# Graph attention over three groups of edges instead of two: weighting half a group later, maxima chained on all 128 partitions, exponentials in a table of their own

## The chip, the cores and the metric

The kernel runs on one core of one Trainium2 chip, as one program. The metric is the device time of one execution in microseconds (us); what is compared is the median of several executions.

## The reference

Four graph layers over 3125 nodes with 256 features and 53125 edges sorted by their destination node. Layers 0 and 1 are normalized sums over edges (GCN). Layer 2 is a graph transformer of three sub-layers, layer 3 a graph attention. The change touches the attention that layer 2 (three times) and layer 3 (once) share, cut here to what matters (8 heads of 32 features):

```python
for l in range(L):                                   # L = 3
    ...
    scores = jnp.sum(q_dst * kt, axis=-1) / scale    # (edges, 8)
    scores = scores * mu[l].T[edge_type]
    m = jax.ops.segment_max(scores, dst, num_segments=N)
    e = jnp.exp(scores - m[dst])
    s = jax.ops.segment_sum(e, dst, num_segments=N)
    w = e / (s[dst] + 1e-10)
    agg = jax.ops.segment_sum(V[src] * w[..., None], dst, num_segments=N)
    attn = agg.reshape(N, D) @ Wo[l] + bo[l]
    x = _layer_norm(x + attn, ...)
    ...                                              # gelu MLP, layer norm
```

Layer 3 computes its scores from other terms, with a leaky relu, and then does the same maximum, exponential and sums.

## The kernel before, in words

**Tiles.** The edges are padded to 464 tiles of 128 edges (NT). Two tiles are a pair that belongs to one block of 128 destination nodes; four tiles are a quad, sixteen tiles (four quads, eight pairs) a group. There are 29 groups (WG). `attend` (L1396) handles all groups in order. It is called four times: `L2a0`, `L2a1`, `L2a2` (together L2a in the profile) and `L3a`.

**What one group needs.** GpSimd (POOL) gathers 16 times 128 rows of the table of keys and values by an indirect DMA (L1460), into a ring of 10 quads (11 in L3a). A slot of the ring is free once its quad has been weighted (`weighted_ready`). SyncE loads the one-hot matrices as bytes; ScalarE (ACT) widens them (`turn` L1709, `widen` L1717). TensorE (PE) multiplies the turned one-hots with the node features (`ask`, L1754, 4 matmuls a quad), which puts each edge's query into PSUM. VectorE (DVE) multiplies by the gathered key (`product`, L1513), reduces over the head (`reduce`, L1519; in L3a `join` adds a gathered term, L1533), and so has 16 x 8 scores.

**The maxima.** PE transposes the scores (`flatten`, L1774). DVE scans them up and down with penalties between segments (`scan_up` L1550, `scan_down` L1555), and spreads the two ends of each tile over a 128 x 32 table (`spread_ends` L1560). PE multiplies this table by `c.head` (128 x 8), so that the ends of all tiles stand in order on 8 partitions (`sequence`, L1779). DVE chains them up and down (`chain_up` L1566, `chain_down` L1572), starting from the group before. PE multiplies by `c.heads` (8 x 128) to spread the result over 128 partitions again (`expand`, L1784). DVE picks each partition's own tile (`pick_own` L1584, `join_own` L1589), raises the scans by it (L1593, L1598) and subtracts (`lower`, L1604). PE transposes back, and computes a factor for sums that started in an earlier group (`unflatten`, L1790 and L1792). ACT takes the exponentials (`soften`, L1729), which it writes straight into the 33rd column of each head of `weighted`, and DVE multiplies the gathered values by them (`weigh`, L1615, once a quad). PE sums each pair with the widened one-hots (`total`, L1765), DVE adds the sums to the accumulator in SBUF (`add`, L1544), and rescales one block (`rescale`, L1625).

**The order.** All is written out by hand: Python loops that are unrolled, one instruction stream for each engine, semaphores between them. In iteration n DVE interleaves the scores of group n with the maxima, the weighting and adds 0 to 2 of group n-1, and adds 3 to 7 of group n-2. After `spread_ends` DVE has one add and one product before `chain_up` waits for `sequence`; after `chain_down` it has a reduction and an add before `pick_own` waits for `expand`; after `lower` it has a product and an add before `weigh` waits for the exponentials. On PE, `total` of pairs 6 and 7 of group n-2 and `ask` of quads 2 and 3 of group n stand between these steps.

## Time and profile before

| | |
|---|---|
| median of 3 runs | 5554.59 us (5538.73 to 5557.21) |
| profiled execution, first to last instruction | 6456.7 us |
| TensorE busy, mean granted clock | 4457.4 us (69%), 0.831 |
| VectorE busy | 3832.0 us (59%) |
| GpSimd busy | 3364.1 us (52%) |
| ScalarE busy | 1605.5 us (25%) |

The profiled execution gives no time of its own beside its span, and the span is 902 us over the median of the runs: this execution was slower than those that are timed. Rows of the profile name an instruction by its source line, its engine, the tensors that it writes and reads, and their shapes; "idle before" is the time in which the engine had nothing to run just before the instruction. The granted clock is TensorE's, as a share of 2.4 GHz. The name of a releaser is inferred; "remote", or a DMA of another stage, stands where it was not found.

### The profile page before, as it was taken

How to read it: one execution, taken by the hardware profiler on the slowest of the kernel's cores; microseconds unless marked ns; L12 is line 12 of the kernel's file. 1: busy time of each engine (PE TensorE's matmuls, PEld its weight loads, DVE VectorE, ACT ScalarE, POOL GpSimd, SP SyncE). 2: the span in 40 equal slices, each digit the busy share in tenths (PEclk: the TensorE clock that was granted, in tenths of full speed). 3: DMA queues.
4: the chain of work that ended last, by engine and by line, in shares of the span. 5: the costliest groups of instructions: out<-in, count | busy, mean ns of one | idle time of the engine just before them, and what ended most of it. 6: DMA issues, size and time to landing. Idle time of an engine off the chain costs nothing. (4 is left out here: it accounts for less than half of the span.)

```text
span 6456.7 us, 68859 instructions
## 1 busy us (share of the span) xinstructions
PE 4457.4 (69%) x19341; PEld 3493.0 (54%) x19341; DVE 3832.0 (59%) x8692; ACT 1605.5 (25%) x3882; POOL 3364.1 (52%) x3108
## 2 busy tenths in 40 slices
PE   5666664577766666778857767796766679766776
PEld 4455453444436455557845555685555558545554
DVE  7544443544455666675347766643766776567777
ACT  3433332200004111113421211243211214312221
POOL 2588886366644555541356555134555530256663
PEclk9888887788888778779977777898778779878887
DMA  3688887255556555542266556315556541256664
GB/s 139 121 124 125 121 125 150 81 184 184 182 165 208 168 173 181 181 144 58 81 189 182 174 175 181 89 56 165 169 175 182 176 147 39 80 168 183 195 192 134
DMA packets 508435, 959.75 MB, mean 149 GB/s; under 512 B 85846, under 2 KB 298020, under 8 KB 507251
## 3 DMA queue, kind: packets, MB, share of 16 engines
q0 software_dynamic: 224512, 549.90, 34.1%
q1 hardware_dynamic: 283426, 404.92, 19.6%
q8 instruction: 170, 2.79, 0.2%
q14 instruction: 199, 1.62, 0.1%
q10 hardware_dynamic: 128, 0.52, 0.0%
HBM read 718.56 MB, written 236.50 MB: 148 GB/s over the span
## 5 line engine op out<-in xcount | busy, mean ns | idle before, releaser
L1460 POOL DMA_INDIRECT L2a_rows<-kv_rows,typed_index x960 | 966.3, 1007 | 627.8 <-DVE L2a_weighted L1615 349.9
L1765 PE MATMUL L2a_sums<-L2a_weighted,L2a_hot 128*128 128x264 f32 x2784 | 830.5, 450 | 166.8 <-DVE L2a_weighted L1615 159.4
L1754 PE MATMUL L2a_query<-x,L2a_turned 128*128 x2784 | 819.8, 447 | 55.8 <-ACT L2a_turned L1709 33.0
L867 POOL DMA_INDIRECT sum_rows<-L0s_rows,L0s_row_of x464 | 724.6, 1562 | 152.9 <-issue 119.4
L1765 PEld LDWEIGHTS L2a_sums<-L2a_weighted,L2a_hot 128*128 128x128 f32 x2784 | 591.2, 221 | 314.5 <-DVE L2a_weighted L1615 186.2
L1754 PEld LDWEIGHTS L2a_query<-x,L2a_turned 128*128 128x128 f32 x2784 | 627.2, 229 | 181.4 <-issue 62.5
L1460 POOL DMA_INDIRECT hold<-kv_rows,typed_index x432 | 445.4, 1031 | 449.8 <-DVE L2a_weighted L1615 279.5
L1460 POOL DMA_INDIRECT L3a_rows<-feature_rows,index x464 | 489.1, 1054 | 301.7 <-DVE L3a_weighted L1615 155.1
L1285 POOL DMA_INDIRECT L1s_rows<-rows,index x464 | 451.0, 972 | 351.2 <-issue 133.8
L1717 ACT ACTIVATE L2a_hot<-L2a_hot 128x512 f32<-128x512 uint8 x348 | 218.7, 629 | 1470.8 <-PE L2a_sums L1765 726.6
L1002 PE MATMUL L0s_message<-features,L0s_share 128*128 x928 | 312.8, 496 | 285.9 <-ACT L0s_share L967 285.9
L2296 POOL TENSOR_SCALAR L2d_here<-hold,mask 128x256 f32<-128x256 f32 x200 | 183.1, 933 | 552.6 <-DVE hold L2372 404.5
L1342 PE MATMUL L1s_code_ps<-L1s_wide,L1s_fields 128*128 128x512 f32 x464 | 285.8, 702 | 219.3 <-DVE L1s_code L1311 138.4
L1519 DVE TENSOR_REDUCE L2a_score<-L2a_prods 128x32 f32<-128x1024 f32 x348 | 417.8, 1201 | 0.4
L1002 PEld LDWEIGHTS L0s_message<-features,L0s_share 128*128 128x128 f32 x928 | 215.3, 242 | 364.9 <-issue 329.1
L1765 PE MATMUL L3a_sums<-L3a_weighted,L3a_hot 128*128 128x264 f32 x928 | 282.7, 457 | 92.6 <-DVE L3a_weighted L1615 89.3
L1709 ACT ACTIVATE L2a_turned<-L2a_turn 128x512 f32<-128x512 uint8 x348 | 216.9, 624 | 507.7 <-PE L2a_query L1754 191.8
L1513 DVE TENSOR_TENSOR L2a_prods<-L2a_query,L2a_rows 128x1024 f32<-128x1024 f32 x240 | 291.9, 1216 | 76.5 <-remote 47.3
L901 DVE TENSOR_TENSOR L0s_hot<-count,early 128x512 f32<-128x512 f32 x116 | 80.5, 694 | 419.0 <-ACT L0s_hot L980 412.7
L1305 DVE TENSOR_TENSOR acc<-acc,L1s_sums 128x256 f32 x232 | 97.4, 420 | 378.4 <-remote 176.5
L1544 DVE TENSOR_TENSOR acc<-acc,L2a_sums 128x264 f32 x696 | 290.4, 417 | 10.8 <-PE L2a_sums L1765 9.1
L1615 DVE TENSOR_TENSOR L2a_weighted<-L2a_rows,L2a_weighted 128x1024 f32<-128x1024 f32 x240 | 292.4, 1218 | 3.4 <-ACT L2a_weighted L1729 1.3
(428 smaller groups left out, 8550.9 us busy)
## 6 DMA issues: line engine op xcount, KB each, us to landing
code_rows<-L1s_code SPq DMA_DIRECT2D x116, 512.0 KB
L3a_code<-code_rows SPq DMA_DIRECT2D x116, 512.0 KB
L0s_wide<-source_rows SPq DMA_DIRECT2D x116, 256.0 KB
L2a_turn<-turned_rows SPq DMA_DIRECT2D x87, 256.0 KB
L2a_pens<-mask_rows SPq DMA_DIRECT2D x87, 256.0 KB
L2a_hot<-hot_rows SPq DMA_DIRECT2D x87, 256.0 KB
kv_rows<-L2d_key_rows SPq DMA_DIRECT2D x50, 384.0 KB, 2.6
kv_rows<-L2d_value_rows SPq DMA_DIRECT2D x150, 128.0 KB, 2.4
```

The lines of the kernel that those rows point to most:

```text
L867: pool.indirect_dma_start(c.sum_rows[u], bass.IndirectOffsetOnAxis(ap=row_of[:, 4 * n + u:4 * n + u + 1], axis=0), rows[n % ring][:, u, :] ...
L1002: last = pe.matmul(message[n % 2][:, u, :], share[n % 2][:, u, :], at(c.q, b[i])[:, 0:D], start=True, stop=True)
L1285: pool.indirect_dma_start(rows[n % ring][:, u, :], None, table, bass.IndirectOffsetOnAxis(ap=c.index[:, t:t + 1], axis=0)).then_inc(landed ...
L1342: pe.matmul(code_ps[j % 2][:, :, :].rearrange("p k d -> p (k d)"), fields[g % 2][:, :], wide[:, 2 * j % FT:2 * j % FT + 2, :].rearrange("p ...
L1460: pool.indirect_dma_start(rows[n % ring][:, u, :], None, table, bass.IndirectOffsetOnAxis(ap=index_of[:, t:t + 1], axis=0)).then_inc(lande ...
L1513: dve.tensor_tensor(prods[q % 2][:, :, :], query[q % 2][:, :, :], other, ALU.mult).then_inc(multiplied, 1)
L1519: last = dve.tensor_reduce(own.rearrange("p k h -> p (k h)"), prods[q % 2][:, :, :].rearrange("p k (h d) -> p (k h) d", h=H), AX.X, ALU.add)
L1544: dve.tensor_tensor(at(c.acc, b), at(c.acc, b), sums[(m * WP + j) % held][:, :], ALU.add).then_inc(added, 1)
L1615: dve.tensor_tensor(weighted[:, 4 * q:4 * q + 4, :].rearrange("p k (h d) -> p k h d", h=H)[:, :, :, 0:HD], rows[quad % ring][:, :, values: ...
L1717: act.activation(hot[quad % 2][:, :, :].rearrange("p u e -> p (u e)"), hot8[m % 2][:, q * 4 * P:(q + 1) * 4 * P], ACT.Copy).then_inc(hot_r ...
L1754: last = pe.matmul(query[q % 2][:, u, :], turned[quad % 2][:, u, :], at(c.q, b[2 * q + u // 2]), start=True, stop=True)
L1765: last = pe.matmul(sums[(m * WP + j) % held][:, :], hot[quad % 2][:, j % 2 * 2 + k, :], weighted[:, 2 * j + k, :], start=k == 0, stop=k == 1)
```

## The change

- `attend` is laid out over three groups. In iteration n (now 31 of them, before 30) DVE makes the scores of group n, the maxima of group n-1 and weights its quads 0 and 1, and weights quads 2 and 3 of group n-2, with all eight adds of that group. The three waits for PE and ACT get more work of DVE in front of them.
- `c.heads` becomes one 128 x 128 matrix (1 where two partitions have the same head), and `sequence` puts the ends on all 128 partitions. The chains run there on 128 x 32 instead of 8 x 32, `pick_own` reads them in SBUF, and `expand` with its two matmul passes is gone. The tables that it needs (`links`, `tail`, `apart`, `ends`) grow from 8 to 128 partitions.
- ACT writes the exponentials into one of two tables `prob`; `pour` (new, one a quad) copies them into `weighted`, which is now one tensor for each quad. `keep` (new) copies the rescaling factor from PSUM to SBUF.
- DVE loads 9 block numbers into registers at the start of an iteration instead of 16.

```diff
-        seq_ps = small[0:H, 2 * P:2 * P + 2 * WT]
-        tops_ps = small[:, 2 * P + 32:2 * P + 32 + 2 * WT]
+        seq_ps = small[:, 2 * P:2 * P + 2 * WT]
...
             def pick_own(m):
-                wait(dve, tops_ready, m + 1)
-                dve.tensor_tensor(pick[:, :, :], tops_ps.rearrange("p (u s) -> p s u", s=2), spread(c.each[:, :], 1, 2),
+                wait(dve, chained, 2 * m + 2)
+                dve.tensor_tensor(pick[:, :, :], tops[:, :].rearrange("p (u s) -> p s u", s=2), spread(c.each[:, :], 1, 2),
                                   ALU.mult).then_inc(picked, 1)
...
             def weigh(m, q):
                 quad = m * WQ + q
                 wait(dve, prob_ready, m + 1)
+                wait(dve, sums_ready, 2 * (quad - WQ + 1))
                 dve.tensor_tensor(
-                    weighted[:, 4 * q:4 * q + 4, :].rearrange("p k (h d) -> p k h d", h=H)[:, :, :, 0:HD],
+                    weighted[q][:, :, :].rearrange("p k (h d) -> p k h d", h=H)[:, :, :, 0:HD],
                     rows[quad % ring][:, :, values:values + D].rearrange("p k (h d) -> p k h d", h=H),
-                    weighted[:, 4 * q:4 * q + 4, HD::HC].unsqueeze(3).broadcast_to([P, 4, H, HD]), ALU.mult
-                ).then_inc(weighted_ready, 1)
+                    spread(prob[m % 2][:, 4 * q:4 * q + 4, :], 3, HD), ALU.mult).then_inc(weighted_ready, 1)
...
             dve.memset(c.acc[:, :, :], 0.0)
-            for n in range(WG + 1):
-                m = n - 1
+            for n in range(WG + 2):
+                m, k = n - 1, n - 2
+                more, chain, tail = n < WG, 0 <= m < WG, k >= 0
...
```

The order of DVE's steps in one iteration after the change, where all three groups are there: product(n,0), add(k,0), scan_up(m), add(k,1), scan_down(m), add(k,2), spread_ends(m), weigh(k,2), reduce(n,0), join(n,0), add(k,3), product(n,1), reduce(n,1), join(n,1), add(k,4), chain_up(m), add(k,5), chain_down(m), grow(m), pick_own(m), join_own(m), reach_first(m), reach_last(m), spread_fall(m), lower(m), weigh(k,3), product(n,2), reduce(n,2), join(n,2), product(n,3), reduce(n,3), join(n,3), add(k,6), add(k,7), weigh(m,0), rescale(m), weigh(m,1). ACT and PE:

```diff
             def soften(m):
-                if m >= 0:
-                    wait(act, below_ready, m + 1)
-                    wait(act, sums_ready, m * WP)
-                    act.activation(weighted[:, :, HD::HC], below_ps.rearrange("p (u h) -> p u h", h=H), ACT.Exp
-                                   ).then_inc(prob_ready, 1)
+                wait(act, below_ready, m + 1)
+                act.activation(prob[m % 2][:, :, :], below_ps.rearrange("p (u h) -> p u h", h=H), ACT.Exp
+                               ).then_inc(prob_ready, 1)
+
+            def pour(m, q):
+                quad = m * WQ + q
+                wait(act, prob_ready, m + 1)
+                wait(act, sums_ready, 2 * (quad - WQ + 1))
+                act.activation(weighted[q][:, :, HD::HC], prob[m % 2][:, 4 * q:4 * q + 4, :], ACT.Copy
+                               ).then_inc(poured, 1)
...
-                pe.matmul(seq_ps, c.head[:, :], ends[:, :, :].rearrange("p u s -> p (u s)"), start=True, stop=True
+                pe.matmul(seq_ps, c.heads[:, :], ends[:, :, :].rearrange("p u s -> p (u s)"), start=True, stop=True
                           ).then_inc(seq_ready, 1)
-
-            def expand(m):
-                wait(pe, chained, 2 * m + 2)
-                pe.matmul(tops_ps, c.heads[:, :], tops[:, :], start=True, stop=True).then_inc(tops_ready, 1)
...
+                    ask(n, 2, now)
+                if tail:
+                    total(k, 3)
                 if chain:
                     sequence(m)
-                total(m - 1, 7)
-                if more:
-                    ask(n, 2, now)
-                if chain:
-                    expand(m)
+                if tail:
+                    total(k, 4)
+                    total(k, 5)
                 if more:
                     ask(n, 3, now)
                 if chain:
                     unflatten(m)
-                total(m, 0)
-                total(m, 1)
+                if tail:
+                    total(k, 6)
+                    total(k, 7)
                 if ahead:
                     ask(n + 1, 0, near)
-                total(m, 2)
-                total(m, 3)
-                if ahead:
                     ask(n + 1, 1, near)
                 if more:
                     flatten(n)
-                total(m, 4)
-                total(m, 5)
-            for j in range(6, WP):
-                total(WG - 1, j)
+                if chain:
+                    total(m, 0)
+                    total(m, 1)
+                    total(m, 2)
```

## Rows read from the trace of the kernel before

**Rows 1.** The page: span, and busy time of each engine.

```profile
span 6456.7 us, 68859 instructions
PE 4457.4 (69%) x19341; PEld 3493.0 (54%) x19341; DVE 3832.0 (59%) x8692; ACT 1605.5 (25%) x3882; POOL 3364.1 (52%) x3108
```

**Rows 2.** Busy time by stretch: first and last call of `attend`, sum of all four.

```profile
core 0: us, PE busy (x) PEld busy (x) DVE busy (x) ACT busy (x) POOL busy (x), PEclk, DMA share, GB/s
2064.00:2911.00 847.00, 573.48 (x2086) 442.55 (x2086) 571.73 (x955) 159.99 (x290) 470.64 (x464) 0.79 0.57 171
...
5611.00:6433.00 822.00, 549.94 (x2086) 427.58 (x2086) 588.52 (x1100) 161.79 (x290) 489.13 (x464) 0.80 0.60 179
sum 3367.00, PE 2269.95 PEld 1754.89 DVE 2303.99 ACT 641.46 POOL 1900.79; mean PE 567.49 PEld 438.72 DVE 576.00 ACT 160.36 POOL 475.20
```

**Rows 3.** Groups of instructions, first L2a, middle (2172 to 2868 us): busy, mean ns, idle before.

```profile
L1460 POOL DMA_INDIRECT L2a_rows<-kv_rows,typed_index x275 | 278.2, 1012 | 188.1 <-DVE L2a_weighted L1615 108.8 <-issue 79.2
L1460 POOL DMA_INDIRECT hold<-kv_rows,typed_index x120 | 124.8, 1040 | 107.0 <-DVE L2a_weighted L1615 73.5 <-issue 33.5
L1566 DVE TENSOR_TENSOR_SCAN L2a_up<-links,L2a_up,L2a_small 8x32 f32<-8x32 f32 x25 | 6.7, 267 | 105.5 <-remote 91.7 <-issue 13.8
L1584 DVE TENSOR_TENSOR L2a_pick<-L2a_small,each 128x32 f32<-128x32 f32 x25 | 4.8, 192 | 98.1 <-DMA raw<-edge_rows 98.1
L1729 ACT ACTIVATE L2a_weighted<-L2a_small 128x128 f32<-128x128 f32 x25 | 10.0, 398 | 22.4 <-PE L2a_small L1792 22.2
L1723 ACT ACTIVATE L2a_fall<-L2a_gap,linked 8x1 f32<-8x1 f32 x25 | 6.9, 278 | 0.0
```

**Rows 4.** The same for L3a, middle (5700 to 6396 us).

```profile
L1460 POOL DMA_INDIRECT L3a_rows<-feature_rows,index x413 | 439.4, 1064 | 251.0 <-DVE L3a_weighted L1615 133.1 <-issue 117.9
L1615 DVE TENSOR_TENSOR L3a_weighted<-L3a_rows,L3a_weighted 128x1024 f32<-128x1024 f32 x104 | 126.9, 1220 | 36.4 <-ACT L3a_weighted L1729 35.9
L1584 DVE TENSOR_TENSOR L3a_pick<-L3a_small,each 128x32 f32<-128x32 f32 x26 | 5.0, 192 | 128.2 <-DMA L2a_rows<-kv_rows,typed_index 107.0 <-issue 21.3
```

**Rows 5.** Timeline, a group early in L2a: start, length, engine, line, [idle before].

```profile
2144.34 0.18 DVE L1560 TENSOR_TENSOR L2a_ends<-each,L2a_most 128x32 f32<-128x32 f32 x1
2144.44 0.42 DVE L1544 TENSOR_TENSOR acc<-acc,L2a_sums 128x264 f32 x1
2144.75 0.22 PE L1779 MATMUL L2a_small<-L2a_ends,head 128*8 128x32 f32 x2
2145.97 1.89 PE L1754 MATMUL L2a_query<-x,L2a_turned 128*128 x8
2153.60 0.27 DVE L1566 TENSOR_TENSOR_SCAN L2a_up<-links,L2a_up,L2a_small 8x32 f32<-8x32 f32 x1 [7.61 <-remote]
2156.59 0.19 DVE L1584 TENSOR_TENSOR L2a_pick<-L2a_small,each 128x32 f32<-128x32 f32 x1 [0.67 <-DMA raw<-edge_rows]
2156.81 0.19 DVE L1589 TENSOR_REDUCE L2a_other<-L2a_pick 128x2 f32<-128x32 f32 x1
2160.13 1.23 DVE L1615 TENSOR_TENSOR L2a_weighted<-L2a_rows,L2a_weighted 128x1024 f32<-128x1024 f32 x1 [0.37 <-ACT L2a_weighted L1729]
```

**Rows 6.** Timeline, the very first group of L2a: the two waits.

```profile
2127.43 0.19 DVE L1584 TENSOR_TENSOR L2a_pick<-L2a_small,each 128x32 f32<-128x32 f32 x1 [1.59 <-PE L2a_small L1784]
2131.79 1.22 DVE L1615 TENSOR_TENSOR L2a_weighted<-hold,L2a_weighted 128x1024 f32<-128x1024 f32 x1 [1.71 <-ACT L2a_weighted L1729]
```

**Rows 7.** Timeline, POOL and DVE a little later: gathers beside a weighting.

```profile
2162.74 1.22 DVE L1615 TENSOR_TENSOR L2a_weighted<-L2a_rows,L2a_weighted 128x1024 f32<-128x1024 f32 x1
2162.87 1.90 POOL L1460 DMA_INDIRECT L2a_rows<-kv_rows,typed_index  x1 [0.30 <-issue]
2165.08 0.95 POOL L1460 DMA_INDIRECT L2a_rows<-kv_rows,typed_index  x1 [0.31 <-issue]
```

**Rows 8.** The page's groups: gathers and scatters of layers 0 and 1.

```profile
L867 POOL DMA_INDIRECT sum_rows<-L0s_rows,L0s_row_of x464 | 724.6, 1562 | 152.9 <-issue 119.4 <-ACT L0s_rows L961 21.9 <-DMA sum_rows<-L0s_rows,L0s_row_of 11.6
L1285 POOL DMA_INDIRECT L1s_rows<-rows,index x464 | 451.0, 972 | 351.2 <-issue 133.8 <-ACTq L87 127.7 <-remote 62.1
```

183 lines of the change are left out of this document (93 added, 90 removed).

## The prediction

> **What bounds the kernel now.** I read the page first: VectorE and GpSimd are busy 59% and 52% of 6456.7 us, TensorE 69% [rows 1], so no engine is the bound by its share. By stretch, the four calls of the attention hold 3367 us of the span, and DVE works 2304 us of them [rows 2]. The groups of one call say where the other 1063 us are. In the middle of L2a, 25 groups of edges take 696 us, 27.8 each. DVE stands idle 105.5 us before the upward chain (L1566) and 98.1 before `pick_own` (L1584), 8.1 us a group, and next to nothing before anything else [rows 3]. In L3a it is 128.2 before `pick_own` and 36.4 before the weighting, 6.3 us a group of 26.4 [rows 4]. Both places wait for a small matmul of TensorE. The timeline shows how such a wait looks: the matmul of `sequence` is recorded at 2144.75 and 0.22 us long, the chain that waits for nothing else starts at 2153.60 [rows 5]. So PE signals far later than its record ends. POOL is no bound in this execution: of 696 us it waits 182 for a weighting to free its ring [rows 3].
>
> The Trainium skill (Perfetto Trace Analysis, Tensor Engine Instruction) says that a matmul's end in a profile is computed from its size, and that its signal comes after PSUM has acknowledged. The 8.6 us between those rows agree that the record does not tell the signal.
>
> **How this execution stands to the timed ones.** Its span is 902 us over the median of 5554.6, and no time of its own stands beside it. I must not book waits that the timed runs don't have. Taking all the waits named out of the attention gives back 84 x 8.14 + 28 x 6.3 = 861 us (28 full groups a call): 3367 - 861 = 2506, and with the 3090 us of everything else 5596. That is 41 us over the median already. So the timed runs have lost most of these waits, and something outside too. What can give outside: POOL's idle time in layer 1, 351.2 less 127.7 ahead of the stage and 464 gaps of 0.30, is 84 us; layer 0's scatters give 44 us if they are 5% shorter [rows 8]; up to 250 us if gathers and scatters are much faster without the profiler. What the timed attention still waits is that sum less 41: 0 to 209 us. From the other side, the waits that are free of the long lag: 0.67 and 0.37 us in a group [rows 5], 1.04 together, or 116 us in 112 groups; 1.59 and 1.71 in the first group [rows 6]. The granted clock is 0.79 in L2a [rows 2], so 42% of the time is at 1.2 GHz; with 3.3 us in that part and 1.04 in the rest it is 2.0 a group, 223 us. I take 150 us, between 116 and the 209 that the balance allows.
>
> **The change part by part.**
>
> *The waits go.* Between `spread_ends` and `chain_up` DVE now has a weighting, a reduction, two adds, a product and another reduction, some 5.7 us where there were 1.5; between `lower` and the weighting two products, two reductions, a weighting and two adds, 6.5 us against 1.5; and `pick_own` waits for DVE alone. PE needs for what stands ahead of `sequence` 8 passes of `ask` (1.89 us) and one `total`, twice that at 1.2 GHz: covered. Removed: -150 us; ends 0 and -209. What is late next is the gather or DVE itself.
>
> *DVE steps that now follow their own input.* Three reductions directly behind their products and `grow` behind the chain; in L3a also three joins behind reductions. Independent neighbours overlap: the add starts at 2144.44 while the one before it ends at 2144.52. Dependent ones don't: `pick_own` ends at 2156.78, the reduction on it starts at 2156.81 [rows 5]. That is 0.11 to 0.12 us a pair: 4 x 0.12 x 84 + 7 x 0.12 x 28 = +64 us, on the path where DVE is the bound, 0 where POOL is. The Trainium skill (VectorE: DVE Perf Modes, The DRAIN you can't avoid) says of copies that a semaphore after each costs nothing extra over one after the last. By that rule this term is 0 and the sum 64 us lower; the rows here show the gap, so I keep it.
>
> *Removed and added small work.* `expand` leaves PE, two short passes off the path. The chains on 128 partitions take what they take on 8: 0.27 for 8 x 32 [rows 3], 0.19 for the 128 x 32 pick [rows 5]. Fewer register loads on DVE and the wider tables of the setup: 0. ACT gets four `pour` and one `keep`, not in the trace: between 0.278 (8 x 1) and 0.398 (128 x 128) each [rows 3], near the lower, 5 x 0.3 = 1.5 us a group on an engine that is busy 641 of 3367 us [rows 2]. That is hidden by the two products and reductions before the weighting; uncovered it would be 0.9 us a group, 100 us. The new waits of `weigh` and `pour` on sums four quads back, and of `flatten` on `keep`, are met an iteration-half earlier; behind them stands all of DVE and, on PE, three `total`. SP's load of the hot bytes of group n now waits for a widening in iteration n, no longer in n-1, and the next turned bytes and, in L3a, the codes are queued behind it. They are needed an iteration later, so 0; if not, see the last rival.
>
> *One more iteration.* After the last product DVE has two weightings and three adds more than now, 2 x 1.13 + 3 x 0.34 = 3.3 us, four times: +13. It costs this because the first groups, from which the work is taken, wait for gathers; else 0.
>
> *POOL.* A gather costs 1.020 + 0.30 us in L2a [rows 3], 1.064 + 0.30 in L3a [rows 4]: 21.1 and 21.8 us a group. DVE without the waits and with the new gaps needs 27.8 - 8.1 + 0.5 = 20.2 and 26.4 - 6.3 + 0.8 = 20.9. By the profile, then, POOL would be the bound after the change. But at that pace the attention alone is 84 x 21.1 + 28 x 21.8 and 293 us of starts and ends, 2676; with 3090 - 128 it is 5638, over the median. The timed gathers must be at least 3% shorter. At 5% they meet DVE's 20.2. I add 10 us for the groups in which POOL is late.
>
> Sum: -150 + 64 + 13 + 10 = -63; 5554.6 - 63 = **5490 us**. Made in the profiled execution's own time the waits are larger: L2a 27.8 to about 21.5, L3a 26.4 to 22, that is 84 x 6.3 + 28 x 4.4 = 652, span about 5805.
>
> **The rivals.**
>
> *The waits are still large in the timed runs.* For it: they are regular, in every group, and the rows name no cause that only a profiler has. Against it: the balance above. Then -209, and the rest as before, less 10 of POOL's lateness: 5554.6 - 209 + 77 = 5423; if the outside gives even more, down to 5380.
>
> *POOL paces the timed runs already.* Then DVE's waits cost nothing now, and removing them nothing: +13 for the tail, 0 for the gaps: 5568, or 5550 if the tail is hidden. For it: POOL's rows sum to over the median. A weighting beside a gather makes it longer: 1.90 against 0.95 us [rows 7]. As a mechanism: where POOL never rests, all four weightings of a group fall on gathers, and POOL's group grows by up to 4 x 0.95. Against it: the timed gathers are shorter by the same sum, and POOL waits 7.3 us a group here [rows 3]. The Trainium skill (GPSIMD Engine Reference, Specifications) says that POOL's SBUF interfaces are shared with VectorE, with contention when a DVE instruction has two SBUF inputs. The weighting has two, and the trace agrees with its 1.90.
>
> *Slower: the ring and the load queue starve.* A gathered quad is held from its product to its weighting. That was 1.2 to 1.6 iterations and becomes 1.6 to 1.85, of a ring that holds 2.5; in L3a ACT, stopped by a turned load that SP issues late, holds back the fall and the pours. Left for waiting, gathering (four of 1.25 us) and landing is 0.65 x 20 = 13 us. It decides when the landing takes more than 8 us. The price is a wait of 1 us a group at the products, 112 us, less half of the 150 removed, plus 77: 5554.6 + 112 - 75 + 77 - 64 (gaps then free) = 5605. For it: 36.4 us of waits for ACT in L3a [rows 4]. Against it: products wait hardly at all now.
>
> That PE's lag exceeds the new cover, so that the change doesn't do what it says, ends with the second rival's time.
>
> **How the numbers follow.** Forecast (5440 to 5540): 0.44. Large waits (5380 to 5440): 0.18. POOL paces (5540 to 5575): 0.22. Starved (5575 to 5640): 0.16. A measurement tells no less than 0.3%, 17 us, from no change: faster is the first two, 0.62, and 0.02 of the third that ends just below the bound; same is the rest of the third, 0.20; slower is the last, 0.16. The range 5385 to 5590 leaves out the tips of both sides.
>
> **What would show it.** In the profile after: idle time of DVE before the chain and `pick_own` under 0.5 us a group; before the weighting under 0.5; L2a groups of 20.5 to 22.5 us; POOL's waits for a weighting under 2 us a group; gathers of 1.0 us or more in the mean; reductions that start 0.03 us after their products. The prediction is wrong if DVE waits at its products for a gather, if `weigh` waits for `pour` or ACT in L3a, or if the span falls by hundreds of us and the timed median does not: then the waits belonged to the profiled execution alone.

## The result and the profile after

The changed kernel takes 5619.27 us (5615.96 to 5623.38), the kernel before beside it 5549.93: ratio 1.0128, 95% interval 1.0114 to 1.0141. It is 1.3% slower, where I forecast 5490, and outside my range.

The profiled execution of before on which the prediction rests was a disturbed one: 902 us over the timed runs, by what, no run shows. So the kernel before was run once more: 5556.04 us, span 5554.4. Its rows and those of the changed kernel (span 5621.7) can be set side by side. Expected of it was:

> The kernel before, unchanged, for a trace of an execution like the timed ones (the first trace spans 6456.7 us, its timed median is 5550). Theory A (gathers pace both): span near 5548, L2a at 20.3 to 20.7 us a group with GpSimd hardly waiting, its start-to-start time per gather below the 1.316 us of the changed kernel. Theory B (VectorE paces the kernel before, and the change made VectorE's group longer): GpSimd waits for weightings 0.5 us a group or more, VectorE idle under 1 us a group. Rival C (the loss is in starts and ends of the four attention calls): groups as long as in the changed kernel, 21.1 and 22.3 us, and the 70 us lie outside the full groups.

First the groups of instructions in the middle of the first L2a (2050 to 2550 us, 24 groups), kernel before, second execution; they answer to [rows 3]. Columns: line, engine, tiles, shapes, count | busy us, mean ns | idle before, released by.

```profile
L1460 POOL DMA_INDIRECT L2a_rows<-kv_rows,typed_index x277 | 277.3, 1001 | 84.5 <-issue 84.5
L1460 POOL DMA_INDIRECT hold<-kv_rows,typed_index x108 | 105.9, 981 | 32.9 <-issue 32.9
L1513 DVE TENSOR_TENSOR L2a_prods<-L2a_query,L2a_rows 128x1024 f32<-128x1024 f32 x68 | 82.7, 1216 | 24.0 <-DMA L2a_rows<-kv_rows,typed_index 21.7 <-issue 1.9
L1566 DVE TENSOR_TENSOR_SCAN L2a_up<-links,L2a_up,L2a_small 8x32 f32<-8x32 f32 x24 | 6.2, 258 | 0.0
L1584 DVE TENSOR_TENSOR L2a_pick<-L2a_small,each 128x32 f32<-128x32 f32 x24 | 4.3, 178 | 0.1
```

The two waits, 8.1 us a group in the first trace, that the change was to remove are 0.0 and 0.1 us in 24 groups together. GpSimd is released by nothing but its own issue: it never waits for a weighting. All 385 gathers with the idle time before them are 500.6 us, 1.300 us each, and 16 of them are the group's 20.8. VectorE waits for gathers at L1513. **The kernel before is paced by GpSimd's gathers**, as theory A had it, whose 20.3 to 20.7 us were a little low. The same lines of the changed kernel:

```profile
L1460 POOL DMA_INDIRECT L2a_rows<-kv_rows,typed_index x272 | 275.4, 1013 | 82.9 <-issue 82.9
L1460 POOL DMA_INDIRECT hold<-kv_rows,typed_index x108 | 109.7, 1015 | 32.9 <-issue 32.9
L1513 DVE TENSOR_TENSOR L2a_prods<-L2a_query,L2a_rows 128x1024 f32<-128x1024 f32 x69 | 83.9, 1216 | 14.0 <-DMA L2a_rows<-kv_rows,typed_index 12.9 <-PE L2a_query L1764 1.1
L1544 DVE TENSOR_TENSOR acc<-acc,L2a_sums 128x264 f32 x189 | 78.9, 417 | 5.5 <-DVE acc L1544 5.1
L1566 DVE TENSOR_TENSOR_SCAN L2a_up<-links,L2a_up,L2a_small 128x32 f32<-128x32 f32 x24 | 6.6, 274 | 0.0
```

Still GpSimd, now at 500.9 / 380 = 1.318 us a gather, 21.1 us a group. In L3a (5000 to 5450 us; [rows 4]) the pace changes hands. Before, then after:

```profile
L1460 POOL DMA_INDIRECT L3a_rows<-feature_rows,index x335 | 348.4, 1040 | 102.1 <-issue 102.1
L1533 DVE TENSOR_TENSOR L3a_score<-L3a_score,L3a_rows 128x32 f32<-128x32 f32 x84 | 15.6, 185 | 29.0 <-DMA L3a_rows<-feature_rows,index 27.0
```

```profile
L1460 POOL DMA_INDIRECT L3a_rows<-feature_rows,index x334 | 322.2, 965 | 128.9 <-issue 96.9 <-DVE L3a_weighted L1616 32.0
L1533 DVE TENSOR_TENSOR L3a_score<-L3a_score,L3a_rows 128x32 f32<-128x32 f32 x82 | 16.4, 200 | 9.2 <-DVE L3a_score L1519 0.9
```

Before, VectorE waits 29.0 us for gathers; after, it hardly does, and GpSimd waits 32.0 us for weightings: VectorE paces, 22.06 us a group instead of the gathers' 21.52 (450.5 / 335 x 16). The busy times by stretch ([rows 2]; L2a, then L3a) agree, before and after:

```profile
2050.00:2550.00 500.00, 422.25 (x1747) 330.32 (x1746) 464.67 (x796) 136.35 (x242) 382.84 (x385) 0.93 0.79 241
5000.00:5450.00 450.00, 370.83 (x1509) 285.91 (x1508) 417.44 (x796) 117.09 (x209) 348.15 (x335) 0.92 0.75 236
```

```profile
2050.00:2550.00 500.00, 407.74 (x1660) 316.56 (x1659) 469.69 (x785) 144.36 (x356) 384.45 (x380) 0.95 0.78 238
5000.00:5450.00 450.00, 353.31 (x1422) 275.29 (x1421) 429.30 (x779) 124.62 (x308) 321.19 (x334) 0.93 0.74 232
```

VectorE's busy time (the third number after the length) rises from 93 to 95% of the stretch in L3a. What the calls of `attend` take, from the starts of the first gather, the last gather and the last addition in the two timelines:

| us, before / after | first to last gather | last gather to last addition ("ends") |
|---|---|---|
| L2a, three calls | 600.9, 602.4, 604.3 / 607.0, 608.5, 609.5 | 27.8, 28.2, 28.0 / 37.5, 39.2, 39.8 |
| L3a | 621.6 / 624.1 | 24.5 / 48.8 |

Gathers +19.9, ends +56.8, together +76.7; outside the attention the changed execution was 9 us quicker, mostly in layer 0, which was not changed. So rival C, a loss in starts and ends, is right about the greater part, though L2a's groups are longer too. The end of the first call, before, then after (VectorE; last gather at 2583.68 and 2580.50):

```profile
2607.05 0.43 DVE L1544 TENSOR_TENSOR acc<-acc,L2a_sums 128x264 f32 x1 [0.19 <-PE L2a_sums L1765]
...
2611.50 0.43 DVE L1544 TENSOR_TENSOR acc<-acc,L2a_sums 128x264 f32 x1 [0.46 <-PE L2a_sums L1765]
```

```profile
2602.31 0.43 DVE L1544 TENSOR_TENSOR acc<-acc,L2a_sums 128x264 f32 x1 [1.36 <-PE L2a_sums L1775]
2603.82 0.43 DVE L1544 TENSOR_TENSOR acc<-acc,L2a_sums 128x264 f32 x1 [1.07 <-PE L2a_sums L1775]
2604.16 1.22 DVE L1616 TENSOR_TENSOR L2a_weighted<-hold,L2a_prob 128x1024 f32<-128x1024 f32 x1
...
2614.49 1.22 DVE L1616 TENSOR_TENSOR L2a_weighted<-L2a_rows,L2a_prob 128x1024 f32<-128x1024 f32 x1
...
2617.06 0.43 DVE L1544 TENSOR_TENSOR acc<-acc,L2a_sums 128x264 f32 x1 [1.36 <-PE L2a_sums L1775]
2617.95 0.43 DVE L1544 TENSOR_TENSOR acc<-acc,L2a_sums 128x264 f32 x1 [0.46 <-PE L2a_sums L1775]
```

After, weightings stand behind additions that wait for TensorE's totals, and the next totals wait for these weightings: the two engines take turns.

**Why 1.300 and not 1.25.** Between two undisturbed gathers lie 1.25 us. Longer ones have a weighting beside them ([rows 7]); here in the changed kernel:

```profile
2301.86 1.22 DVE L1616 TENSOR_TENSOR L2a_weighted<-L2a_rows,L2a_prob 128x1024 f32<-128x1024 f32 x1
2302.69 1.20 POOL L1460 DMA_INDIRECT hold<-kv_rows,typed_index  x1 [0.30 <-issue]
2302.99 1.21 DVE L1519 TENSOR_REDUCE L2a_score<-L2a_prods 128x32 f32<-128x1024 f32 x1
...
2304.20 0.95 POOL L1460 DMA_INDIRECT hold<-kv_rows,typed_index  x1 [0.30 <-issue]
2304.46 1.21 DVE L1513 TENSOR_TENSOR L2a_prods<-L2a_query,hold 128x1024 f32<-128x1024 f32 x1
```

The first gather starts 0.39 us before the weighting's end and is 0.25 longer than the second, beside which a product runs. Over the stage a gather that starts in a weighting is longer by the rest of the weighting less 0.12 us. Summed over a group that is 0.74 us before and 1.02 after in L2a: the whole difference between 1.300 or 1.318 and 1.254 us a gather.

### The profile page after: what moved, and what is told of

It is laid out like the page before. It is cut to its first block and busy times, and to the rows that moved or that the text cites. A ratio compares the mean times of both kernels' runs of the same rounds, so it can differ in the third digit from the quotient of the medians.

```text
span 5621.7 us, 70778 instructions
## 1 busy us (share of the span) xinstructions
PE 4193.5 (75%) x19108; PEld 3301.3 (59%) x19108; DVE 3887.3 (69%) x8691; ACT 1677.0 (30%) x4458; POOL 3323.8 (59%) x3108
## 5 line engine op out<-in xcount | busy, mean ns | idle before, releaser
L1775 PE MATMUL L2a_sums<-L2a_weighted,L2a_hot 128*128 128x264 f32 x2784 | 781.5, 430 | 119.0 <-DVE L2a_weighted L1616 118.3
L1764 PE MATMUL L2a_query<-x,L2a_turned 128*128 x2784 | 717.3, 406 | 153.2 <-DVE L2a_prods L1513 115.0
L1764 PEld LDWEIGHTS L2a_query<-x,L2a_turned 128*128 128x128 f32 x2784 | 547.2, 203 | 313.6 <-issue 236.5
L1775 PEld LDWEIGHTS L2a_sums<-L2a_weighted,L2a_hot 128*128 128x128 f32 x2784 | 558.5, 208 | 260.3 <-DVE L2a_weighted L1616 167.8
L1460 POOL DMA_INDIRECT L3a_rows<-feature_rows,index x464 | 447.5, 964 | 191.0 <-issue 147.7
L1460 POOL DMA_INDIRECT hold<-kv_rows,typed_index x432 | 434.0, 1005 | 179.6 <-issue 179.6
L1352 PE MATMUL L1s_sums<-L1s_rows,L1s_hot 128*128 128x256 f32 x928 | 258.7, 404 | 125.4 <-issue 106.4
L1352 PEld LDWEIGHTS L1s_sums<-L1s_rows,L1s_hot 128*128 128x128 f32 x928 | 177.1, 199 | 288.7 <-issue 233.5
L1513 DVE TENSOR_TENSOR L2a_prods<-L2a_query,L2a_rows 128x1024 f32<-128x1024 f32 x240 | 291.9, 1216 | 77.7 <-DMA L2a_rows<-kv_rows,typed_index 76.6
L1775 PE MATMUL L3a_sums<-L3a_weighted,L3a_hot 128*128 128x264 f32 x928 | 269.0, 441 | 43.0 <-DVE L3a_weighted L1616 42.8
L1616 DVE TENSOR_TENSOR L2a_weighted<-L2a_rows,L2a_prob 128x1024 f32<-128x1024 f32 x240 | 291.3, 1214 | 0.1
```

What stands on the lines that cost most here:

```text
L1352: last = pe.matmul(sums[j % held][:, 0:D], hot[n % hots_held][:, u, :], rows[n % ring][:, u, :], start=k == 0, stop=k == 1)
L1460: pool.indirect_dma_start(rows[n % ring][:, u, :], None, table, bass.IndirectOffsetOnAxis(ap=index_of[:, t:t + 1], axis=0)).then_inc(lande ...
L1513: dve.tensor_tensor(prods[q % 2][:, :, :], query[q % 2][:, :, :], other, ALU.mult).then_inc(multiplied, 1)
L1616: dve.tensor_tensor(weighted[q][:, :, :].rearrange("p k (h d) -> p k h d", h=H)[:, :, :, 0:HD], rows[quad % ring][:, :, values:values + D] ...
L1764: last = pe.matmul(query[q % 2][:, u, :], turned[quad % 2][:, u, :], at(c.q, b[2 * q + u // 2]), start=True, stop=True)
L1775: last = pe.matmul(sums[(m * WP + j) % held][:, :], hot[quad % 2][:, j % 2 * 2 + k, :], weighted[j // 2][:, j % 2 * 2 + k, :], start=k == ...
```

## The experiments

Ratios are to the kernel before, run beside them, with 95% intervals. In the code cuts `...` marks what is left out; a moved line is shown at its new place alone, without the `if` lines around it.

**The parts alone.** Only the chains on 128 partitions:

```diff
-        up = [st.sb(f"up{k}", [H, 2 * WT]) for k in range(2)]
+        up = [st.sb(f"up{k}", [P, 2 * WT]) for k in range(2)]
-                if chain:
-                    expand(m)
```

> The kernel before with only the chains moved to 128 partitions: the maxima are no longer spread back by a matmul, the own ones are picked from SBUF. Theory A (in the kernel before POOL issues gathers without ever waiting for a weighting, at 1.300 us a gather in L2a and 1.348 in L3a, so it alone sets a group's 20.8 and 21.6 us, and a wait taken from VectorE buys nothing): ratio 0.999 to 1.001 against the kernel before (5545 to 5556 us). Theory P (the prediction's: the two waits of 7 to 8 us in each group are on the path, and this part takes one of them): 5470 to 5510 us. Theory S (the parts themselves cost, the picked maxima now a VectorE operation on SBUF behind its predecessor): 5560 to 5590 us.

5551.50 us, 1.0007 (0.9998 to 1.0016). Theory A holds: a wait taken from an engine that does not pace is worth nothing.

Only the table of exponentials, `pour` and `keep`:

```diff
-                    weighted[:, 4 * q:4 * q + 4, HD::HC].unsqueeze(3).broadcast_to([P, 4, H, HD]), ALU.mult
+                    spread(prob[m % 2][:, 4 * q:4 * q + 4, :], 3, HD), ALU.mult).then_inc(weighted_ready, 1)
-                    ... spread(shrink_ps, 2, HC), 1.0, heads(at(c.acc, b)),
+                    ... spread(shrink[:, :], 2, HC), 1.0, heads(at(c.acc, b)),
```

> The kernel before with only the exponentials in a table of their own, four small copies into the weighted rows and the shrink factors copied to SBUF, in the old order of two groups. Theory A: POOL still sets the pace, the weightings still read two SBUF operands; only the rescaling now reads two as well and can stretch one more gather a group by up to 0.25 us, so 0 to +20 us: 5550 to 5570 us, and the gather start to start is 1.300 to 1.31 us in L2a. Theory P: the wait of the exponentials for the totals goes, 5480 to 5530 us. Theory S (four more copies on ScalarE delay the widened hot rows and so the totals): over 5575 us with VectorE waiting for totals.

5572.65 us, 1.0038 (1.0024 to 1.0051), gathers at 1.317 to 1.323 us in L2a: theory A's cause, but a little over both of its ranges. The same with the factor of the rescaling left in PSUM:

```diff
-                    ... spread(shrink[:, :], 2, HC), 1.0, heads(at(c.acc, b)),
+                    ... spread(shrink_ps, 2, HC), 1.0, heads(at(c.acc, b)),
-                    keep(m)
```

> The kernel before with the exponentials in a table of their own (the run that took 5573 us), but with the rescaling reading the shrink factors from PSUM as before, so that one SBUF operand less stands in the chain. Theory A (the 23 us which the table cost are gathers stretched by rescaling and weighting in a row, both with two SBUF operands, 0.3 us a group): back to 5545 to 5558 us, the gather at 1.300 to 1.306 us. Theory S (the table's cost is the weighting that reads the table, or the copies on ScalarE): stays at 5565 to 5578 us.

5553.64 us, 1.0004 (0.9993 to 1.0014), 1.300 to 1.308 us. The edit takes away both the rescaling's second SBUF operand and `keep`; the trace with the table tells the two apart (the rescaling is L1627):

```profile
2396.86 1.24 DVE L1618 TENSOR_TENSOR L2a_weighted<-hold,L2a_prob 128x1024 f32<-128x1024 f32 x1
2398.03 0.42 DVE L1627 SCALAR_TENSOR_TENSOR acc<-L2a_shrink,acc 128x264 f32 x1
2398.10 1.17 POOL L1462 DMA_INDIRECT hold<-kv_rows,typed_index  x1 [0.30 <-issue]
...
2399.50 1.21 DVE L1618 TENSOR_TENSOR L2a_weighted<-L2a_rows,L2a_prob 128x1024 f32<-128x1024 f32 x1
2399.57 1.96 POOL L1462 DMA_INDIRECT hold<-kv_rows,typed_index  x1 [0.30 <-issue]
```

A gather held to the end of the rescaling brings the next one to 0.07 us after the start of the next weighting, where it is held for 1.01 us. Of 63 groups in the middles of L2a's calls 14 show this; with the factor in PSUM none does, though 8 gathers start in a rescaling. In the old order the table's cost is the rescaling's second SBUF operand. Both parts together, that is the chains' edit and the table's with `keep`:

> Both parts (chains on 128 partitions, exponentials in a table) in the old order of two groups, without the third group in flight. Theory A with C (the loss of the changed kernel, 69 us, comes from the layout over three groups: 33 us from the additional iteration's end in L2a, 27 in L3a and the rest from three SBUF-SBUF operations in a row): 5550 to 5572 us, the last gather to the last addition stays at 28 us a call. Theory S (the parts are the cause, the layout costs nothing): 5605 to 5630 us.

5569.21 us, 1.0032 (1.0020 to 1.0044): theory A with C, and not S. So 18 us of the loss come with the parts in the old order, some 53 (1.0128 less 1.0032) with the layout.

**Weightings with one SBUF operand.** The kernel before, with the exponentials left in PSUM:

```diff
-                    weighted[:, 4 * q:4 * q + 4, HD::HC].unsqueeze(3).broadcast_to([P, 4, H, HD]), ALU.mult
+                    spread(below_ps.rearrange("p (u h) -> p u h", h=H)[:, 4 * q:4 * q + 4, :], 3, HD), ALU.mult
...
-                    act.activation(weighted[:, :, HD::HC], below_ps.rearrange("p (u h) -> p u h", h=H), ACT.Exp
-                                   ).then_inc(prob_ready, 1)
+                    act.activation(weighted[:, :, HD::HC], below_ps.rearrange("p (u h) -> p u h", h=H), ACT.Exp)
+                    act.activation(below_ps, below_ps, ACT.Exp).then_inc(prob_ready, 1)
...
-                wait(pe, rescaled, n - 1)
+                wait(pe, weighted_ready, n * WQ)
```

> The kernel before with the exponentials taken in place in PSUM, from where the weightings read them, so that a weighting has one SBUF operand only, as a product has; one more exponential of 0.3 us a group on ScalarE, and the transpose of the scores waits for the group's last weighting. Theory A (a gather whose start falls into a weighting is held until about that weighting's end, because both of its operands are in SBUF, and this is all that lies between 1.300 or 1.348 us and 1.251): 1.25 to 1.26 us a gather in L2a, 20.0 to 20.2 us a group instead of 20.8, in L3a 20.1 to 20.9 instead of 21.6; 5455 to 5500 us. Theory R (the stretch comes from any VectorE work on SBUF, or from the write): no change, 5545 to 5556 us. Theory Q (reading the weights from PSUM makes the weighting itself longer, over 1.1 us, and VectorE becomes the bound): 5570 us or more.

5460.35 us, 0.9841 (0.9828 to 0.9854): theory A. The groups of its middle of L2a:

```profile
L1460 POOL DMA_INDIRECT L2a_rows<-kv_rows,typed_index x280 | 265.9, 950 | 85.3 <-issue 84.7 <-DVE L2a_weighted L1615 0.6
L1460 POOL DMA_INDIRECT hold<-kv_rows,typed_index x119 | 113.1, 950 | 36.3 <-issue 36.0 <-DVE L2a_weighted L1615 0.3
L1615 DVE TENSOR_TENSOR L2a_weighted<-L2a_rows,L2a_small 128x1024 f32<-128x1024 f32 x70 | 84.3, 1205 | 0.4
```

1.2546 us a gather. The mean has come down from 1001 to 950 ns, and the weighting costs no more than before. A gather that starts in a weighting now passes at full speed:

```profile
2309.17 1.22 DVE L1615 TENSOR_TENSOR L2a_weighted<-L2a_rows,L2a_small 128x1024 f32<-128x1024 f32 x1
2309.74 0.95 POOL L1460 DMA_INDIRECT L2a_rows<-kv_rows,typed_index  x1 [0.30 <-issue]
```

By the rule of 0.12 us it would have been held for 0.53. With the first edit, the chains on 128 partitions, besides:

> The exponentials in place in PSUM (as in the run that took 5460 us) and beside them the chains on 128 partitions, old order of two groups. With POOL's gathers at 1.254 us the group in L2a has 0.6 us of VectorE's idle time left and that in L3a none (VectorE busy 19.93 of 20.24 us). Theory A: in L2a nothing (POOL paces), in L3a the maxima's spreading back was never waited for, so nothing: 5450 to 5470 us. Theory P (once POOL is out of the way, the waits taken from the chain count): 5420 to 5445 us.

**5452.19 us, 0.9818 (0.9804 to 0.9833): the quickest version, 1.8% below the kernel before.** In this run's L3a a group takes 20.1 us of VectorE's time instead of 20.2, and the end of that call 7 us less, while the gathers are as fast. Its interval and that of the run without the chains (0.9828 to 0.9854) overlap, so whether the chains bring these 8 us I leave open.

**The ends of the calls.** In the changed kernel, the last group's weightings 2 and 3 (its third and fourth) at the head of the additional iteration:

```diff
+                if tail and not chain:
+                    weigh(k, 2)
+                    weigh(k, 3)
```

> The changed kernel, with the last group's two late weightings issued ahead of its additions in the additional iteration. Theory C (the drain is 37 to 40 us from the last gather to the last addition instead of 28, since the additions of the last two groups alternate with weightings, each of which TensorE must wait for): 3 to 8 us less in each call of L2a and in L3a, 5589 to 5607 us in all, mid-stage groups unchanged at 21.1 and 22.06 us. Theory D (the drain is long since the sums are bound by TensorE's three accumulators and VectorE's additions, not by the weightings' place): 5615 to 5622 us.

5625.81 us, 1.0129 (1.0112 to 1.0146): no gain that can be told, below what theory C asked for. The ends are 38.0, 36.3, 33.5 and 45.6 us, 12 us less in all; in the trace the same turns are still taken one iteration earlier, by the group before the last.

**VectorE's order.** The products' sums, the joins and weighting 3 put between the steps of the chain, so that hardly a step follows its own input (and the same ends as above):

```diff
                     chain_up(m)
+                    join(n, 1)
                     chain_down(m)
...
                     pick_own(m)
+                    weigh(k, 3)
                     join_own(m)
+                    product(n, 2)
                     reach_first(m)
+                    reduce(n, 2)
                     reach_last(m)
+                    join(n, 2)
```

> As the one with the drain shortened, and VectorE's order of the changed kernel reshuffled so that no operation but one stands directly behind the one it depends on (sums and folds of the products go between the steps of the chain). Theory B (L3a is bound by VectorE in the changed kernel: 21.04 us of work and 1.0 us between dependent neighbours in a group of 22.06): a group in L3a comes down to 21.1 to 21.5 us, or 16 to 27 us in the stage; in L2a, where POOL sets the pace at 1.319 us a gather, the group stays at 21.1. With the drain 5565 to 5592 us. Theory P2 (the gaps between dependent operations are on L2a's path too, as the prediction booked them at 0.12 us a pair): another 0.5 us a group of L2a, 5525 to 5555 us.

5697.47 us, 1.0265 (1.0249 to 1.0280), over 100 us above what I expected. With the last additions moved back, and the ends as in the changed kernel:

```diff
                     reduce(n, 3)
                     join(n, 3)
+                    add(k, 6, blocks[6])
                     weigh(m, 0)
+                    add(k, 7, blocks[7])
                     weigh(m, 1)
+                        rescale(m, blocks[8])
```

> The changed kernel with VectorE's order reshuffled once more: hardly an operation behind the one it depends on, and the last two additions later, one ahead of and one behind a weighting, so that TensorE has brought their totals (in the first reshuffling they waited 2.5 us a group for them). Theory B (L3a of the changed kernel is VectorE's 21.8 us of work and dependent gaps a group; spaced it needs 20.0): a group in L3a 21.1 to 21.6 us instead of 22.06, then set by POOL's stretched gathers (1.33 to 1.35 us), 13 to 27 us less; in L2a 21.0 to 21.2 as before it. In all 5588 to 5612 us. Theory E (TensorE's chain of totals, not VectorE's order, holds L3a): waits of VectorE for sums of over 0.5 us a group remain and the time is 5615 us or more.

5688.23 us, 1.0259 (1.0245 to 1.0273): slower by 70 us where I expected a gain. VectorE's busy time a group in L3a did fall, from 21.0 to 20.2 us, as theory B has it. But, as theory E has it, VectorE now waits for sums: TensorE, whose program is in order, stands before `unflatten` until the drawn-out chain is done. Its waits in the latter kernel, L2a, and the stretch (PE first, clock behind POOL):

```profile
PE L2a_small L1807 <- DVE L2a_zz L1604: 105.5, 23, 4.9
```

```profile
2050.00:2550.00 500.00, 394.40 (x1572) 324.79 (x1571) 442.36 (x748) 137.14 (x339) 389.07 (x365) 0.88 0.76 228
```

That is 4.6 us a group, where the changed kernel waits 1.8 (42.9 in 24 groups). The granted clock, a mean of stretches at 2.4 and at 1.2 GHz, is 0.88 instead of 0.95, and VectorE waits 2.0 us a group for totals and at no product for a gather. How much of these 2.0 us is the late start and how much the clock, no run tells. A third version with the ends and the rescaling mended too took 5686.53 us, 1.0252, where I had expected 5535 to 5565. The order that keeps the chain in one piece and separates only the pairs outside it:

```diff
                     reduce(n, 0)
+                    product(n, 1)
                     join(n, 0)
...
                     reduce(n, 2)
+                    product(n, 3)
                     join(n, 2)
...
                     reduce(n, 3)
+                    add(k, 6, blocks[6])
                     join(n, 3)
```

> The changed kernel with VectorE's order changed outside the chain alone: a product, an addition or a weighting stands between most sums of products and what needs them; the chain's operations stay behind one another and as early as they were. Theory B (L3a is bound by VectorE's work and by 0.1 to 0.2 us between dependent neighbours): six such pairs a group fewer in L3a, so 0.7 to 1.1 us a group less than 22.06 and 19 to 30 us less in that stage; in L2a, where POOL paces, within 0.1 us a group: 5588 to 5604 us. Theory E (TensorE's totals bound L3a): VectorE's wait for sums grows by what the gaps lose, 5612 to 5625 us.

5604.07 us, 1.0093 (1.0078 to 1.0108): 19 us less than the changed kernel by the ratios, 15 by the medians. L3a, same window:

```profile
L1460 POOL DMA_INDIRECT L3a_rows<-feature_rows,index x341 | 348.1, 1021 | 103.9 <-issue 103.6 <-DVE L3a_weighted L1616 0.3
L1533 DVE TENSOR_TENSOR L3a_score<-L3a_score,L3a_rows 128x32 f32<-128x32 f32 x86 | 15.6, 182 | 13.3 <-DMA L3a_rows<-feature_rows,index 13.2
```

GpSimd waits 0.3 us instead of 32.0 and paces again, 21.1 to 21.2 us a group. Theory B holds for L3a. With the late weightings ahead of the additions in both last iterations:

```diff
+                if tail and not more:
+                    weigh(k, 2)
+                    weigh(k, 3)
```

> As the one with the pairs separated, and in the last two iterations of each call the late weightings ahead of the additions. Theory C (the last two groups' additions wait for totals which wait for weightings queued behind additions): from the last gather to the last addition 30 to 35 us a call in L2a instead of 37 to 40, and 8 to 12 us less in L3a, 20 to 30 us in all below the one with the pairs alone: 5560 to 5582 us. Theory D (TensorE's own totals, 0.9 us each for a group and a half, are the drain's length): within 8 us of the one with the pairs alone.

5584.56 us, 1.0057 (1.0044 to 1.0071), another 20 us, as theory C asked, though 3 above the range I gave. The ends are 33.5, 33.3, 33.8 and 30.1 us.

**What sets L2a's 1.32.** The changed kernel with its rescaling from PSUM, the same edit as in the old order:

> The changed kernel with the rescaling reading the shrink factors from PSUM as before the change; the next transpose of the scores waits for it. Theory A (0.3 us a group of L2a is the rescaling's second SBUF operand between two weightings): gather pace in L2a 1.300 to 1.307 us instead of 1.319, 17 to 25 us less in three calls, 5592 to 5606 us; L3a, where VectorE paces, stays at 22.06. Theory F (the weightings next to each other stretch gathers whatever the rescaling reads; or the wait of the transpose costs as much): 5612 to 5625 us.

5630.80 us, 1.0155 (1.0141 to 1.0169): nothing back, 6 us above theory F's range, 1.316 to 1.325 us a gather, and L3a's group 22.3. What explained the table in the old order does not explain the new one. One weighting moved in the kernel before:

```diff
                 if chain:
+                    weigh(m, 1)
+                if more:
                     reduce(n, 2)
```

> The kernel before with one operation moved: the second weighting of a group stands directly behind the rescaling, ahead of the sum of the products that stood between them. The four weightings then start 1.5, 3.9 and 2.6 us apart instead of 2.6, 2.7 and 2.6. Theory G (a gather that starts in a weighting is held until that weighting's end; with starts a little over two gathers of 1.25 us apart the next gathers meet the next weighting late and lose 0.1 us each, with other distances 0.2 to 0.4 us): gather pace in L2a from 1.300 to 1.310-1.320 us, 0.15 to 0.3 us a group, 5560 to 5578 us. Theory H (the sum of the stretches does not depend on the weightings' distances): 5543 to 5555 us and 1.300 to 1.304.

5545.28 us, 0.9990 (0.9981 to 1.0000): H by the time. The traces lie between: 1.303, 1.309 and 1.308 us a gather in the middles of the L2a calls (before 1.300, 1.300 and 1.307), 1.343 in L3a (before 1.345). The second weighting's stretch rose from 0.08 to 0.22 us, the third's and fourth's fell from 0.29 to 0.14 together, and the first's rose from 0.38 to 0.52. In the changed kernel, `reduce(n, 3)` between the last two weightings:

```diff
                     rescale(m, blocks[8])
+                    reduce(n, 3)
+                    join(n, 3)
                     weigh(m, 1)
```

> The changed kernel with one operation moved: the sum of the group's last products goes between the rescaling and the weighting behind it, so that the last two weightings start 2.65 us apart instead of 1.5. Theory G: the fourth weighting's stretch falls from 0.2 to 0.1 us and the gather pace in L2a to 1.305 to 1.315 us, 5 to 17 us less over three calls, 5602 to 5614 us; L3a, paced by VectorE, as it was. Theory H: 5615 to 5625 us at 1.318 to 1.321.

5635.03 us, 1.0142 (1.0122 to 1.0161), 1.320 us in L2a: no gain, so H rather than G, but 10 us above H's range. In L3a GpSimd no longer waits, but runs at 1.37.

The traces say more than either theory. A held gather is followed by the next one 1.13 us after the weighting's end (0.95 + 0.30 - 0.12), and then one starts every 1.25 us. So the distance from the end of one weighting to the start of the next says how far into that one a gather starts, and how long it is held. Counted for each of some 60 groups in the middles of L2a's three calls, then averaged (the 0.74 and 1.02 us above are the first call's):

| weighting of the group | first | second | third | fourth | sum |
|---|---|---|---|---|---|
| before: distance, us | 11.70 | 1.39 | 1.51 | 1.39 | |
| held, counted so / measured | 0.42 / 0.38 | 0.10 / 0.08 | 0.21 / 0.21 | 0.10 / 0.10 | 0.82 / 0.76 |
| changed: distance, us | 6.64 | 0.26 | 2.80 | 6.56 | |
| held, counted so / measured | 0.36 / 0.36 | 0.23 / 0.22 | 0.26 / 0.26 | 0.25 / 0.22 | 1.10 / 1.05 |

The difference of 0.3 us a group is that between 1.300 and 1.318 us a gather: the old order left 1.39 to 1.51 us between weightings, which lets two gathers pass and leaves the next a short hold. In the last run above the second weighting stands at 1.39 us too, but is measured at 0.19 and not 0.10: in 6 of 63 groups the rescaling ahead of it, with its two SBUF operands, had held a gather and shifted the next.

Last, the test on the whole layout. A PSUM bank had to be freed, so its control is the version of 5584.56 us with two banks for the sums instead of three (`held, codes = 2, 4`):

> Control: the changed kernel with the pairs separated and the drain mended (the run that took 5585 us), but two instead of three PSUM banks for the sums, so that TensorE waits for the addition two pairs back. Steady groups in L2a are paced by POOL and have 0.9 us of VectorE's idle time left: 0 to +40 us, 5580 to 5625 us; gather pace still 1.318 to 1.325 us in L2a unless VectorE has become the bound.

5642.55 us, 1.0169 (1.0155 to 1.0183), 18 us over my range: 1.346 to 1.355 us a gather. VectorE waits 0.44 us for a sum, so weighting 2, the group's third, starts 1.95 instead of 1.41 us after the upward scan's start, 3.34 instead of 2.80 us after the weighting before it, and each time meets a gather early:

```profile
2304.08 1.22 DVE L1616 TENSOR_TENSOR L2a_weighted<-L2a_rows,L2a_prob 128x1024 f32<-128x1024 f32 x1
2304.37 1.75 POOL L1460 DMA_INDIRECT hold<-kv_rows,typed_index  x1 [0.30 <-issue]
```

Held for 0.80 us, once a group, instead of 0.26; the count above gives 0.80 too. With the exponentials in the freed bank:

```diff
+            def show(m):
+                wait(act, prob_ready, m + 1)
+                wait(act, weighted_ready, m * WQ)
+                act.activation(prob_ps, prob[m % 2][:, :, :], ACT.Copy).then_inc(shown, 1)
...
-                    spread(prob[m % 2][:, 4 * q:4 * q + 4, :], 3, HD), ALU.mult).then_inc(weighted_ready, 1)
+                    spread(prob_ps[:, 4 * q:4 * q + 4, :], 3, HD), ALU.mult).then_inc(weighted_ready, 1)
```

> As the control, with the freed bank used for a copy of the exponentials in PSUM, which the weightings read, so that they have one SBUF operand. Theory A (all stretching of gathers comes from the weightings' two SBUF operands, in this layout as in the old): gathers at 1.251 to 1.258 us in L2a, and VectorE or POOL paces at 20.1 to 20.5 us a group instead of 21.1; 45 to 80 us below the control. Theory J (part of the pace is the layout's own): pace stays over 1.27 us, less than 40 us below the control.

5541.10 us, 0.9982 (0.9973 to 0.9991): 101 us below its control, more than I gave it.

```profile
L1461 POOL DMA_INDIRECT L2a_rows<-kv_rows,typed_index x273 | 258.9, 948 | 90.0 <-issue 78.9 <-DVE L2a_weighted L1617 11.1
L1545 DVE TENSOR_TENSOR acc<-acc,L2a_sums 128x264 f32 x195 | 82.1, 421 | 16.0 <-PE L2a_sums L1788 10.5 <-DVE acc L1545 5.1
```

Theory A holds for the gathers: all stretching is gone. GpSimd even waits for weightings (11.1 us here), and VectorE, with its waits for sums, paces at 20.6 us a group. In this layout too, what L2a's gathers lost above 1.25 us was due to the weightings' two SBUF operands. Against the 5460 us of the same cure in the old order the layout still loses some 80 us; how much of that is the two banks was not tried.

## Why the prediction was wrong

**The waits (-150).** The step that failed. In the second execution of the kernel before they are 0.1 us in 24 groups together: worth 0, the end that I had allowed and not taken; and taking one of them away alone changed nothing (1.0007). The lag between a matmul's record and its successor [rows 5] belonged to the first execution alone; in the second the matmul is recorded, in the last group of the first call, at 2595.62, 0.23 us long, and the chain starts at 2595.88:

```profile
2595.62 0.23 PE L1779 MATMUL L2a_small<-L2a_ends,head 128*8 128x32 f32 x2
2595.88 0.27 DVE L1566 TENSOR_TENSOR_SCAN L2a_up<-links,L2a_up,L2a_small 8x32 f32<-8x32 f32 x1 [0.72 <-PE L2a_small L1779]
```

So the 8.6 us, from which I read that a matmul's record does not tell its signal, were a lag of that one execution: here it is 0.03 us. I let the outside of the attention give up to 250 us, which no run shows (it gave 73, 3017 us for 3090), and took 150 us of waits from short ones of 1.04 us in the disturbed timeline. Where GpSimd sets the time, a wait less before one step is a wait more at the products.

**GpSimd.** I had its 21.1 and 21.8 us a group from rows and dismissed them, since they summed to more than the median. They are 20.8 and 21.5: 1.4% off. The error in that sum was in the starts and ends of the calls. I took them over from the disturbed execution at 293 us; in the second they are 188 (the four calls' 2537 less 84 x 20.8 and 28 x 21.5). So "at least 3% shorter" gathers did not follow. The rival "POOL paces already" had the right mechanism, a chance of 0.22, and 51 us too little. The weighting beside a gather stood there as its evidence [rows 7], but not as a price that a new order could raise. The Trainium skill (GPSIMD Engine Reference, Specifications) names the contention with VectorE instructions of two SBUF inputs; the runs agree: taking it away is worth 1.6% of the kernel before.

**Dependent neighbours (+64).** Kind and size right, place wrong. In L3a I had 24 us for seven new pairs. Separating six pairs, five of these seven and one that the old order had as well, gave back 19 for the whole kernel. The 40 us of L2a are not there: GpSimd paces, and VectorE's idle time before its products only shrank.

**The additional iteration (+13).** A mis-sized term: 3.3 us a call by busy times, 9.7 to 11.8 in L2a and 24.3 in L3a by the timelines. I summed what VectorE executes there and not the turns it takes with TensorE. In L3a VectorE's lag behind the gathers is in it too: its last product starts 12.7 us after the last gather. What was mended in both last iterations gave 20 us.

**POOL's lateness (+10).** +20 us of gathers, by another cause: more time held by weightings.

**Small work 0, chains 0.** Right for the chains (1.0007) and the copies; wrong for `keep`, which gives the rescaling a second SBUF operand that costs 18 to 21 us in the old order. The slower rival, starvation of ring and load queue, did not happen: in 500 us of L2a VectorE waits 17.8 us for gathers at its products, before 28.3 (the DMA parts of L1513, with `hold`).

The loss, then, by ratios: 18 us the parts, 19 the pairs, 20 the ends, 14 left. By the traces the ends are still 5 to 6 us a call longer, 22 in all, and L3a's gathers 11 us shorter (611.1 for 621.6). In that sum the 18 are what the parts cost in the old order; in the new one the operand alone gave nothing back, though the pace is the same 1.32. There the distances between the weightings account for the pace, as the table above counts; no order with better distances was tried in the new layout.

My list of signs caught it: VectorE waits at its products for gathers, and the span fell by 835 us where the median did not.

## What to carry to other kernels

If the profiled execution is hundreds of us over the timed ones, take another before booking any wait from it; until then trust steady rates (16 gathers a group, here right to 1.4%) over idle times. Ask first whether one queue issues without ever waiting for data: then only its own rate matters, and what stretches its instructions is worth more than any wait elsewhere, and a new order changes where the stretching instructions fall. Before an order is loosened, look at what the in-order engines behind it wait for: six pairs separated outside the chain gained 19 us, while work put between the chain's own steps lost 70.

## What the runs showed of the hardware

An indirect gather that starts inside a VectorE tensor_tensor with two SBUF inputs (128x1024, fp32, 1.22 us) is held until that instruction's end: its record is 1.75 us when it starts 0.29 into it, 1.20 at 0.83, 0.95 undisturbed. The rescaling (128x264, 0.42 us, two SBUF inputs) holds one too: 1.17 us at 0.07 into it. With one input in PSUM the weighting holds nothing, and takes 1205 to 1212 ns in L2a instead of 1211 to 1213. The Trainium skill (SBUF — State Buffer, SBUF: two separate sides) describes the shared pair of ports as an exclusive lock, which VectorE takes with two SBUF inputs only against a GpSimd instruction that reads SBUF. The runs agree that the gather waits for the instruction's end and that PSUM lifts it. They do not show the lock the other way round: a weighting that starts while a gather has run for over 0.1 us takes 1.21 us as ever, and the gather its 0.95.
